# A recurrent cross-attention kernel: one pre-activation bank, dense matmuls at the loop's entry and unread matmul columns in every step

## The chip, the cores and the metric

The kernel runs on one core of a Trainium2 chip. The number that counts is the device time of one execution in microseconds. Three runs of the kernel before gave 1774.48, 1775.82 and 1776.86 us; the median is 1775.82 us.

## What is computed

Two layers act on `x` (4 sequences x 256 positions x 512). Each layer is an attention block and a feed-forward block with residual additions. The first attention block, the dequantized feed-forward block of the first layer and the routed experts of the second are large matrix products. The second layer's attention block is a recurrence over the 256 positions, and it is what the change touches. For each batch row (4) it attends over 64 context positions of 128 features:

```python
def step(carry, tgt):
    s, c, alpha = carry
    f = conv(alpha, conv_w)                                   # 101 taps, 10 channels
    e = einsum('a,bta->bt', va, tanh(enc_proj + (s @ Wa_s.T)[:, None, :] + f @ Wa_f + ba))
    alpha_new = softmax(where(mask, e, -1e30))
    g = einsum('bt,btd->bd', alpha_new, hbatch)
    y = ...                                                   # computed after the loop from kept s and alpha
    rec = tgt @ L_ys.T + s @ L_ss.T + g @ L_gs_w.T + L_gs_b
    ig, fg, cg, og = split(rec)
    c_next = sig(fg) * c + sig(ig) * tanh(cg)
    s_next = sig(og) * tanh(c_next)
```

Each step needs the state `s` and the attention weights of the step before, so 256 steps stand one behind the other.

## The kernel before

The kernel is written engine by engine: each engine has its own instruction list, and counting semaphores (`wait_ge`, `then_inc`) tie them together. Nothing schedules it; the order on each engine is the order of the code. TensorE runs first the attention block, two passes of `gate_up` and `down` for the first feed-forward block with the recurrence's input products in between, then the recurrence loop `pe.Fori(0, S // 2)` with two steps in each turn (`par` 0 and 1, 256 steps in all), and then the expert block.

The numbers of a step in the code, in TensorE's order:

- **The pre-activation** (bank `par`, 128 columns): `context_part` puts the context projection and bias there with three matmuls against the identity (L1181), the convolved attention weights come on top with two float32 matmuls over `uh` and `qv` (L1243), which appear in the trace as four weight loads and four matmuls, and the state part `was2` with `sh` twice and `sl` once (L1193). The state is held in two half-precision pieces, `sh` (high) and `sl` (low). `context_part` and L1243 of step l prepare step l+1: they write bank `1 - par` while the step's own tanh read bank `par`.
- **The state's part of the gates** (L1199): ten matmuls of 4 columns, independent of the attention.
- ScalarE takes tanh of the pre-activation twice (L955 for the high piece `th_hi`, L956 in full precision); VectorE forms the low piece (L746). TensorE forms the scores in bank 2 (L1206, eight matmuls in 32-row groups of outputs, for the maximum, which VectorE reduces at L749) and in bank 3 (L1211, L1213).
- ScalarE's exp (L960, `eh`; L961 in float32), then TensorE's sums over the context: gates (L1221), normaliser (L1227, L1231), and the transform of the attention weights (L1236, L1237). The masks for the next step (L1175, L1176) and `context_part` (L1181) follow at once; they wait for nothing.
- VectorE: reciprocal (L755), products (L760, L769), gate sum `gat` (L771), then two `spread` products (L764), which L1243 waits for (`q0_ready`, `q1_ready`). ScalarE's L963, L964 and L966 and VectorE's L778, L780, L783 make the new state; `sh` releases the next step's L1193, and `sl` (L786) its third matmul.

GpSimd keeps the history (L490, L493) and splits expert weights in the loop. In the trace some names are those of the storage that a tile shares: `krep` stands for `qv` and for the context's gate projection `hg2`, `interT` for the tanh tiles, `s` and `sscale` for the history.

Of the kernel before, what the change touches and what calls it, by code (L numbers as in the profile page):

```python
# [8 lines left out]
ACT = mybir.ActivationFunctionType  # L9
# [7 lines left out]
P = 128  # L17
B, S, H = 4, 256, 512
# [9 lines left out]
J = 64  # L28
KW = 101
FCH = 10  # L30
TH = T // 2
# [46 lines left out]
def build(nc, a, out):  # L78
    with ExitStack() as ctx:
# [32 lines left out]
        identb = sb("identb", [P, P], BF16)  # L112
# [9 lines left out]
        was2 = sb("was2", [J, 2, P], F16)  # L122
# [10 lines left out]
        uh = sb("uh", [P, 2, P])  # L133
        enc = sb("enc", [P, P])
        enc3 = sb("enc3", [P, 3, P], BF16)
# [20 lines left out]
        th = interT[:, 6, 0:P]  # L156
# [686 lines left out]
        def _(act):  # L843
# [107 lines left out]
            with act.Fori(0, S // 2) as i:  # L951
                for par in range(2):
                    l = i * 2 + par
                    act.wait_ge(s["pre_done"], l + 1)
                    nc.scalar.activation(th_hi, bank[par][:, 0:P], ACT.Tanh).then_inc(s["th_s"], 1)  # L955
                    nc.scalar.activation(th, bank[par][:, 0:P], ACT.Tanh).then_inc(s["th_full"], 1)  # L956

                    act.wait_ge(s["et_done"], l + 1)
                    act.wait_ge(s["mx_ready"], l + 1)
                    nc.scalar.activation(eh[:], bank[3][:, 0:8], ACT.Exp, bias=nmx[:, 0:1]).then_inc(s["eh_ready"], 1)  # L960
                    nc.scalar.activation(ex[:, par, :], bank[3][:, 0:8], ACT.Exp, bias=nmx[:, 0:1]).then_inc(s["ex_ready"], 1)  # L961
                    act.wait_ge(s["g_ready"], l + 1)
                    nc.scalar.activation(xs[:, par, 4:12], gat[J:P, :], ACT.Tanh, scale=0.5)  # L963
                    nc.scalar.activation(tfi[:], gat[0:J, :], ACT.Tanh, scale=0.5).then_inc(s["tg_ready"], 1)  # L964
                    act.wait_ge(s["c_ready"], l + 1)
                    nc.scalar.activation(tc_sb[:], xs[:, 1 - par, 0:4], ACT.Tanh, scale=0.5).then_inc(s["tc_ready"], 1)  # L966
# [34 lines left out]
        def _(pe):  # L1001
            mm = nc.tensor.matmul
# [160 lines left out]
                        pass  # L1163

            down(2 * IT0, IT0, wd, B, last_gates)
            pe.wait_ge(s["setup_v"], 1)
            pe.wait_ge(s["mask_ready"], 1)
            pe.wait_ge(s["rin_ready"], 2 * B)
# [6 lines left out]
                mm(bank[2][:, 0:T], bsel[:], maskb[:], start=True, stop=False, skip_group_check=True)  # L1175
                mm(bank[3][:, 0:8], etl[:], etr[:], start=True, stop=False, skip_group_check=True)  # L1176

            def context_part(par):

                for j in range(3):  # L1180
                    mm(bank[par][:, 0:P], identb[:], enc3[:, j, :], start=(j == 0), stop=False, skip_group_check=True)  # L1181

            masks()
            context_part(0)

            with pe.Fori(0, S // 2) as i:
                for par in range(2):
# [2 lines left out]
                    state_part = [(0, sh), (1, sh), (0, sl)]  # L1190
                    for j, st in state_part:
                        pe.wait_ge(s["sl_ready" if st is sl else "sh_ready"], l + 1)
                        last = mm(bank[par][:, 0:P], was2[:, j, :], st[:].unsqueeze(2).broadcast_to([J, B, TH]),  # L1193
                                  start=False, stop=(st is sl), skip_group_check=True)
                    last.then_inc(s["pre_done"], 1)

# [3 lines left out]
                                      start=(j == 0 and st is sh), stop=(j == 1 and st is sl))  # L1200
                    last.then_inc(s["sp_done"], 1)

                    pe.wait_ge(s["th_s"], l + 1)
                    for b in range(B):
                        for h in range(2):
# [6 lines left out]
                    pe.wait_ge(s["th_lo_ready"], l + 1)  # L1212
                    mm(bank[3][:, 0:8], th_lo, vae2[:, 0, :], start=False, stop=True, skip_group_check=True).then_inc(s["et_done"], 1)  # L1213

                    pe.wait_ge(s["eh_ready"], l + 1)

                    def gates(parts, e, first, final):
# [18 lines left out]
                        mm(bank[7][:, 0:8], fwd[:, j, :], eh[:], start=(j == 0), stop=False)  # L1236
                    mm(bank[7][:, 0:8], fwd[:, 0, :], el[:], start=False, stop=True).then_inc(s["ah_done"], 1)  # L1237
                    masks()
                    context_part(1 - par)

                    for h in range(2):
                        pe.wait_ge(s[f"q{h}_ready"], l + 1)
                        mm(bank[1 - par][:, 0:P], uh[:, h, :], qv[:, h, :, :], start=False, stop=False, skip_group_check=True)  # L1243


            pe.wait_ge(s["hist_done"], S)
# [86 lines left out]
```

## Time and profile before

| what | value |
|---|---|
| median of three runs (lowest, highest) | 1775.82 us (1774.48, 1776.86) |
| span of the profiled execution | 1777.0 us, 43152 instructions |
| TensorE busy, weight loads busy | 1506.0 us (85%), 1022.2 us (58%) |
| VectorE, ScalarE, GpSimd busy | 919.2 us (52%), 528.9 us (30%), 387.5 us (22%) |
| recurrence loop, from the first mask matmul to the first matmul behind it | 444.8 to 1603.6 us |
| granted TensorE clock, mean over the span | 0.633 of full speed |

The profile gives no other time for its execution than the span, which is 1.2 us above the median of the runs. The kernel has three stages: up to 444 us the dense part, then 1159 us of recurrence, then some 173 us of experts and output. The page is read by stage: a share of the whole span mixes the three. [...]

### The profile page before, as it was taken

The numbers are of one execution on the slowest core, as the hardware profiler recorded it, in microseconds if no ns is written. First come the engines' busy times: TensorE is split into PE (matmuls) and PEld (weight loads), VectorE is DVE, ScalarE is ACT, GpSimd is POOL, SyncE is SP. The second block draws the span as 40 slices with busy tenths as digits, with TensorE's granted clock in tenths as the row PEclk, the third lists the DMA queues.
The fourth block names the chain that finished last, engine by engine and source line by source line (L and its number), as shares of the span: only waits on it lengthen the run. The fifth ranks groups of instructions, "written<-read, shape, count | busy, mean of one in ns | idle before, by whom it ended". The sixth has DMA issues, their size and how long they took to land.

```text
span 1777.0 us, 43152 instructions
## 1 busy us (share of the span) xinstructions
PE 1506.0 (85%) x15683; PEld 1022.2 (58%) x15683; DVE 919.2 (52%) x4293; ACT 528.9 (30%) x2023; POOL 387.5 (22%) x1030
## 2 busy tenths in 40 slices
PE   6547999999888888888888888888888888887999
PEld 3334454544666666666666666666666666664443
DVE  4996643331555555555555555555555555553422
ACT  1342231221333333333333333333333333331211
POOL 3344321220000222222222222222222222222211
PEclk7658999999555555555555555555555555555999
DMA  8330000001200000000000000000000000000000
GB/s 326 141 115 11 1 1 0 1 1 52 77 0 0 0 0 0 0 0 0 0 0 0 0 0 0 0 0 0 0 0 0 0 0 0 0 0 1 1 24 25
DMA packets 17363, 34.51 MB, mean 19 GB/s; under 512 B 7476, under 2 KB 8675, under 8 KB 17332
## 3 DMA queue, kind: packets, MB, share of 16 engines
q1 hardware_dynamic: 17332, 34.10, 5.3%
q8 instruction: 20, 0.33, 0.1%
q14 instruction: 11, 0.09, 0.0%
HBM read 32.00 MB, written 2.10 MB: 19 GB/s over the span
## 4 chain that ended last, share of the span: by engine, by line
PE 62%; DVE 25%; issue 6%; ACT 5%; POOL 1%; DVEq 1%; SPq 1%; DMA 0%; POOLq 0%; ACTq 0%
PE bank L1243 18%; PE bank L1073 11%; PE bank L1193 6%; PE bank L1088 6%; PE bank L1221 5%; ACT eh L960 4%; DVE interT L746 4%; PE bank L1199 4%; DVE krep L764 3%; PE bank L1213 3%; DVE rinv L755 3%; DVE rs L743 2%; DVE g L760 2%; PE bank L1231 2%; DVE gat L771 2%
## 5 line engine op out<-in xcount | busy, mean ns | idle before, releaser
L1243 PE MATMUL bank<-krep,uh 128*128 128x128 f32 x1024 | 313.1, 461 | 23.6
L1243 PEld LDWEIGHTS bank<-krep,uh 128*128 128x128 f32 x1024 | 237.4, 320 | 92.4 <-DVE krep L764 92.4
L493 POOL TENSOR_TENSOR sscale<-ex,rinv 128x8 f32 x256 | 51.3, 200 | 667.6 <-DVE rinv L755 667.6
L1221 PE MATMUL bank<-eh,krep 128*128 128x4 f16 x2048 | 95.3, 168 | 92.5 <-ACT eh L960 92.5
L764 DVE TENSOR_TENSOR krep<-inv,ahn 128x128 f32<-128x128 f32 x512 | 162.2, 356 | 0.0
L1073 PE MATMUL bank<-xT,wbig 128*128 128x512 f16 x672 | 157.2, 386 | 3.7 <-DVE xT L591 3.7
L743 DVE TENSOR_TENSOR rs<-bank,rin 128x8 f32<-128x8 f32 x256 | 42.8, 167 | 198.1 <-PE bank L1199 198.1
L1221 PEld LDWEIGHTS bank<-eh,krep 128*128 128x128 f16 x2048 | 74.1, 105 | 114.0 <-ACT eh L960 114.0
L963 ACT ACTIVATE xs<-gat 64x8 f32<-64x8 f32 x256 | 53.4, 208 | 288.7 <-DVE gat L771 288.7
L955 ACT ACTIVATE interT<-bank 128x128 f16<-128x128 f32 x256 | 71.2, 278 | 216.9 <-PE bank L1193 216.9
L1181 PE MATMUL bank<-enc,identb 128*128 128x128 bf16 x771 | 128.4, 303 | 0.0
L752 DVE TENSOR_TENSOR el<-ex,eh 128x8 f16<-128x8 f32 x256 | 43.0, 168 | 155.9 <-ACT ex L961 155.9
L1088 PE MATMUL bank<-wbig,interT 128*128 128x512 f16 x504 | 115.5, 387 | 1.4 <-POOL interT L449 1.4
L960 ACT ACTIVATE eh<-bank,nmx 128x8 f16<-128x8 f32 x256 | 68.7, 268 | 155.7 <-PE bank L1213 155.7
L1073 PEld LDWEIGHTS bank<-xT,wbig 128*128 128x128 f16 x672 | 67.0, 102 | 83.3 <-issue 13.5
L1199 PEld LDWEIGHTS bank<-sh,lss 64*128 64x128 bf16 x1536 | 102.4, 114 | 0.0
L1199 PE MATMUL bank<-sh,lss 64*128 64x4 f16 x1536 | 101.3, 170 | 0.0
L1193 PE MATMUL bank<-sh,was 64*128 64x128 f16 x512 | 100.0, 297 | 0.0
L490 POOL COPY sscale<-s 64x4 f32 x256 | 46.4, 181 | 242.8 <-DVE s L784 242.8
L652 DVE SCALAR_TENSOR_TENSOR act_sb<-tanh_sb,bank 128x512 f32<-128x512 f32 x42 | 28.9, 687 | 128.5 <-ACT tanh_sb L895 128.4
L449 POOL TENSOR_TENSOR interT<-act_sb,interT 128x512 f16<-128x512 f32 x42 | 48.9, 1165 | 207.8 <-ACT interT L884 207.8
L1206 PE MATMUL bank<-interT,vah 128*32 128x32 f16 x2048 | 65.5, 198 | 31.3
(201 smaller groups left out, 3044.5 us busy)
## 6 DMA issues: line engine op xcount, KB each, us to landing
wbig<-d_gate_qT SPq DMA_DIRECT2D x4, 896.0 KB, 10.1
wbig<-d_up_qT SPq DMA_DIRECT2D x4, 896.0 KB, 20.7
wbig<-d_down_qT SPq DMA_DIRECT2D x1, 3584.0 KB, 30.5
d_out<-x_sb SPq DMA_DIRECT2D x8, 256.0 KB, 2.0
sscale<-d_gate_sT SPq DMA_DIRECT2D x2, 896.0 KB, 8.6
interT<-d_gate_sT SPq DMA_DIRECT2D x2, 896.0 KB, 14.9
sscale<-d_up_sT SPq DMA_DIRECT2D x2, 896.0 KB, 4.2
interT<-d_up_sT SPq DMA_DIRECT2D x2, 896.0 KB, 4.3
```

The source lines that it names most:

```text
L743: nc.vector.tensor_tensor(rs[:].unsqueeze(1), bank[6][:, 0:8].unsqueeze(1), rin2[:, bass.ds(i, 1), par, :], ALU.add)
L746: nc.vector.tensor_tensor(th_lo, th, th_hi, ALU.subtract).then_inc(s["th_lo_ready"], 1)
L764: return nc.vector.tensor_tensor(qv[:, h, :, :], inv[:].unsqueeze(1).broadcast_to([P, B, TH]), ahn[:, 4 * h:4 * h + 4].unsqueeze(2).broadc ...
L955: nc.scalar.activation(th_hi, bank[par][:, 0:P], ACT.Tanh).then_inc(s["th_s"], 1)
L960: nc.scalar.activation(eh[:], bank[3][:, 0:8], ACT.Exp, bias=nmx[:, 0:1]).then_inc(s["eh_ready"], 1)
L1073: last = mm(bk[:], w[wi][:, kt, it * P:(it + 1) * P], x[xi][:, kt, :], start=(kt == 0 and wi + xi == 0), stop=(kt == KT - 1 and xi == 1))
L1088: last = mm(bank[6 + b % 2][:], i_part[ii][:, it, b * CL:(b + 1) * CL], w[wi][:, it, :], start=(it == 0 and ii + wi == 0), stop=(it == til ...
L1181: mm(bank[par][:, 0:P], identb[:], enc3[:, j, :], start=(j == 0), stop=False, skip_group_check=True)
L1193: last = mm(bank[par][:, 0:P], was2[:, j, :], st[:].unsqueeze(2).broadcast_to([J, B, TH]), start=False, stop=(st is sl), skip_group_check= ...
L1199: last = mm(bank[6][:, 4 * gp:4 * gp + 4], lss3[:, j, gp * P:(gp + 1) * P], st[:], start=(j == 0 and st is sh), stop=(j == 1 and st is sl))
L1221: ins = mm(bank[4][:, 4 * gp:4 * gp + 4], hg2[:, j, h, gp * P:(gp + 1) * P], e[:, 4 * h:4 * h + 4], start=(first and gp == 0 and j == 0 an ...
L1243: mm(bank[1 - par][:, 0:P], uh[:, h, :], qv[:, h, :, :], start=False, stop=False, skip_group_check=True)
```

## The change

Three things change, all on TensorE except the bank that ScalarE reads.

```diff
-                    nc.scalar.activation(th_hi, bank[par][:, 0:P], ACT.Tanh).then_inc(s["th_s"], 1)
-                    nc.scalar.activation(th, bank[par][:, 0:P], ACT.Tanh).then_inc(s["th_full"], 1)
+                    nc.scalar.activation(th_hi, bank[0][:, 0:P], ACT.Tanh).then_inc(s["th_s"], 1)
+                    nc.scalar.activation(th, bank[0][:, 0:P], ACT.Tanh).then_inc(s["th_full"], 1)
...
             down(2 * IT0, IT0, wd, B, last_gates)
+
+            for _ in range(16):
+                mm(bank[1][:], x_part[0][:, 0, 0:P], x_part[0][:, 0, :], start=True, stop=True)
             pe.wait_ge(s["setup_v"], 1)
...
+            def keep_busy(n):
+
+                mm(bank[1][:, 0:n], identb[:], hg2[:, 0].rearrange("p h g -> p (h g)")[:, 0:n], start=True, stop=True)
...
-                        last = mm(bank[par][:, 0:P], was2[:, j, :], st[:].unsqueeze(2).broadcast_to([J, B, TH]),
+                        last = mm(bank[0][:, 0:P], was2[:, j, :], st[:].unsqueeze(2).broadcast_to([J, B, TH]),
...
+                    keep_busy(256)
                     pe.wait_ge(s["th_s"], l + 1)
...
+                    keep_busy(256)
                     pe.wait_ge(s["eh_ready"], l + 1)
...
                     masks()
-                    context_part(1 - par)
+                    context_part()
+                    keep_busy(256)
 
                     for h in range(2):
                         pe.wait_ge(s[f"q{h}_ready"], l + 1)
-                        mm(bank[1 - par][:, 0:P], uh[:, h, :], qv[:, h, :, :], start=False, stop=False, skip_group_check=True)
+                        mm(bank[0][:, 0:P], uh[:, h, :], qv[:, h, :, :], start=False, stop=False, skip_group_check=True)
+                    keep_busy(512)
```

The pre-activation has one bank, bank 0, for all steps. Bank 1 takes results that nothing reads: 16 matmuls of 512 columns between the last input product and the loop, and four `keep_busy` matmuls in each step, of 256, 256, 256 and 512 columns, against the identity. None of them waits for a semaphore. The lists of the other engines keep their order.

TensorE's list at the loop's entry, before; L1009 and L1111 are the last input transposes and products of the recurrence:

```order
L1009 MATMUL bank<-ident,xn 128x128 x4
L1111 MATMUL bank<-sscale,lys 128x128 x8
L1175 MATMUL bank<-maskb,bsel 128x64
L1176 MATMUL bank<-etr,etl 128x8
L1181 MATMUL bank<-enc,identb 128x128 x3
L1186 UNCONDITIONAL_BRANCH
```

And after, where lines 1175, 1176, 1181 and 1186 have become 1178, 1179, 1184 and 1193:

```order
L1009 MATMUL bank<-ident,xn 128x128 x4
L1111 MATMUL bank<-sscale,lys 128x128 x8
L1168 MATMUL bank<-xT 128x512 x16
L1178 MATMUL bank<-maskb,bsel 128x64
L1179 MATMUL bank<-etr,etl 128x8
L1184 MATMUL bank<-enc,identb 128x128 x3
L1193 UNCONDITIONAL_BRANCH
```

The sixteen stand ahead of the semaphore waits that precede the masks. TensorE's list from a step's `context_part` over the step's end into the next step's state part, before:

```order
L1176 MATMUL bank<-etr,etl 128x8
L1181 MATMUL bank<-enc,identb 128x128 x3
L1243 MATMUL bank<-krep,uh 128x128 x2
L1192 REGISTER_ALU
L1193 MATMUL bank<-sh,was 128x128 x2
L1193 MATMUL bank<-sl,was 128x128
L1199 MATMUL bank<-sh,lss 128x4 x3
```

And after (L1188 is `keep_busy`):

```order
L1179 MATMUL bank<-etr,etl 128x8
L1184 MATMUL bank<-enc,identb 128x128 x3
L1188 MATMUL bank<-krep,identb 128x256
L1253 MATMUL bank<-krep,uh 128x128 x2
L1188 MATMUL bank<-krep,identb 128x512
L1199 REGISTER_ALU
L1200 MATMUL bank<-sh,was 128x128 x2
L1200 MATMUL bank<-sl,was 128x128
L1206 MATMUL bank<-sh,lss 128x4 x3
```

The third unread matmul stands between the context part and the float32 pair, the fourth between that pair and the matmuls that the new state releases. TensorE's list around the scores, before:

```order
L1199 MATMUL bank<-sl,lss 128x4 x2
L1206 MATMUL bank<-interT,vah 32x32 x8
L1211 MATMUL bank<-vae,interT 128x8 x2
L1213 MATMUL bank<-vae,interT 128x8
L1221 MATMUL bank<-eh,krep 128x4 x8
```

And after:

```order
L1206 MATMUL bank<-sl,lss 128x4 x2
L1188 MATMUL bank<-krep,identb 128x256
L1214 MATMUL bank<-interT,vah 32x32 x8
L1219 MATMUL bank<-vae,interT 128x8 x2
L1221 MATMUL bank<-vae,interT 128x8
L1188 MATMUL bank<-krep,identb 128x256
L1230 MATMUL bank<-eh,krep 128x4 x8
```

The first unread matmul stands ahead of the wait for tanh, the second ahead of the wait for exp.

## Rows read from the trace of the kernel before

**Rows 1.** The page's forty slices: tenths of full clock, by slice of 44.4 us.

```profile
PEclk7658999999555555555555555555555555555999
```

**Rows 2.** Busy time by stretch: us, each engine's busy time (instructions), clock, DMA share, GB/s.

```profile
26.00:40.00 14.00, 13.35 (x45) 9.99 (x45) 5.10 (x8) 3.81 (x8) 2.08 (x2) 0.50 1.01 420
...
330.00:400.00 70.00, 70.00 (x331) 32.50 (x329) 18.96 (x31) 16.39 (x32) 15.09 (x13) 1.00 0.00 1
...
445.00:446.50 1.50, 1.24 (x29) 0.92 (x27) 0.56 (x3) 0.45 (x2) 0.00 (x0) 1.00 1.03 406
446.50:450.00 3.50, 3.04 (x36) 2.35 (x37) 1.81 (x12) 1.05 (x5) 0.39 (x2) 0.51 1.01 376
...
600.00:1600.00 1000.00, 851.58 (x11500) 646.29 (x11499) 547.66 (x3316) 332.02 (x1549) 214.57 (x774) 0.50 0.00 0
...
1636.00:1641.00 5.00, 5.00 (x11) 1.45 (x11) 0.00 (x0) 0.00 (x0) 0.00 (x0) 0.50 0.00 0
1641.30:1650.00 8.70, 8.70 (x31) 3.04 (x30) 3.38 (x7) 1.28 (x2) 0.94 (x3) 1.00 0.00 0
```

**Rows 3.** Timeline of all engines, one step's state part, scores and exp: start, us, what.

```profile
703.92 0.28 ACT L955 ACTIVATE interT<-bank 128x128 f16<-128x128 f32 x1 [0.85 <-PE bank L1193]
703.94 0.19 PE L1199 MATMUL bank<-sl,lss 64*128 64x4 f16 x2
...
704.25 0.26 PE L1206 MATMUL bank<-interT,vah 128*32 128x32 f16 x8
...
704.61 0.22 DVE L749 TENSOR_REDUCE nmx<-bank 128x1 f32<-128x64 f32 x1
...
704.75 0.19 PE L1213 MATMUL bank<-vae,interT 128*128 128x8 f16 x1
704.98 0.27 ACT L960 ACTIVATE eh<-bank,nmx 128x8 f16<-128x8 f32 x1 [0.61 <-PE bank L1213]
```

**Rows 4.** The same timeline, the same step's later part and the next step's state part.

```profile
705.30 0.37 PE L1221 MATMUL bank<-eh,krep 128*128 128x4 f16 x8 [0.36 <-ACT eh L960]
...
706.16 0.50 PE L1181 MATMUL bank<-enc,identb 128*128 128x128 bf16 x3
...
706.76 0.92 PEld L1243 LDWEIGHTS bank<-krep,uh 128*128 128x128 f32 x4 [0.36 <-DVE krep L764]
706.76 1.22 PE L1243 MATMUL bank<-krep,uh 128*128 128x128 f32 x4
...
707.63 0.15 DVE L783 SCALAR_TENSOR_TENSOR sh<-xs,tc_sb 64x4 f16<-64x4 f32 x1 [0.27 <-ACT tc_sb L966]
...
707.91 0.13 PEld L1193 LDWEIGHTS bank<-sh,was 64*128 64x128 f16 x2 [0.23 <-DVE sh L783]
...
708.10 0.30 PE L1193 MATMUL bank<-sl,was 64*128 64x128 f16 x1
```

**Rows 5.** One line's matmuls at low clock (600 to 1590 us): duration ns min/median/max.

```profile
L1193 PE MATMUL bank<-sl,was x218: 293/304/309, 604.1 to 1585.7; 64*128 64x128 f16 x109
...
L1181 PE MATMUL bank<-enc,identb x657: 287/311/311, 602.1 to 1588.5; 128*128 128x128 bf16 x165
```

**Rows 6.** The same lines at full clock (444 to 447 us).

```profile
L1193 PE MATMUL bank<-sl,was x1: 213/213/213, 445.3 to 445.3; 64*128 64x128 f16 x1
```

**Rows 7.** Timeline at the loop's entry: the last input product, the first masks, the first scores and exp.

```profile
441.58 2.05 PE L1111 MATMUL bank<-sscale,lys 128*128 128x128 f32 x16 [0.69 <-ACT sscale L912]
...
444.82 0.18 PE L1175 MATMUL bank<-maskb,bsel 4*128 4x64 bf16 x1 [1.18 <-issue]
...
445.59 0.28 ACT L955 ACTIVATE interT<-bank 128x128 f16<-128x128 f32 x1 [0.99 <-PE bank L1193]
...
446.64 0.27 ACT L960 ACTIVATE eh<-bank,nmx 128x8 f16<-128x8 f32 x1 [0.60 <-PE bank L1213]
```

**Rows 8.** Dense stages, TensorE timeline: 512-column matmuls, at full clock and at the low one.

```profile
427.27 9.65 PE L1088 MATMUL bank<-wbig,interT 128*128 128x512 f16 x42
...
1636.32 4.02 PE L1073 MATMUL bank<-wbig 128*128 128x512 f16 x9
```

More of the change, by code:

```diff
@@ L1176, in masks, with context_part @@
                 mm(bank[3][:, 0:8], etl[:], etr[:], start=True, stop=False, skip_group_check=True)
-            def context_part(par):
+            def context_part():
                 for j in range(3):
-                    mm(bank[par][:, 0:P], identb[:], enc3[:, j, :], start=(j == 0), stop=False, skip_group_check=True)
+                    mm(bank[0][:, 0:P], identb[:], enc3[:, j, :], start=(j == 0), stop=False, skip_group_check=True)
+            def keep_busy(n):
+                mm(bank[1][:, 0:n], identb[:], hg2[:, 0].rearrange("p h g -> p (h g)")[:, 0:n], start=True, stop=True)
             masks()
-            context_part(0)
+            context_part()
             with pe.Fori(0, S // 2) as i:
@@ L1238, in _ @@
                     masks()
-                    context_part(1 - par)
+                    context_part()
+                    keep_busy(256)
                     for h in range(2):
                         pe.wait_ge(s[f"q{h}_ready"], l + 1)
-                        mm(bank[1 - par][:, 0:P], uh[:, h, :], qv[:, h, :, :], start=False, stop=False, skip_group_check=True)
+                        mm(bank[0][:, 0:P], uh[:, h, :], qv[:, h, :, :], start=False, stop=False, skip_group_check=True)
+                    keep_busy(512)
             pe.wait_ge(s["hist_done"], S)
```

## The prediction

> **What bounds the kernel now.** I read first the page's slices of the granted clock, then busy time by stretch, then the timeline of one step.
>
> The slices show three stages [rows 1]: mixed clock up to slice 8, about half of full speed (1.2 GHz) through the loop, full speed (2.4 GHz) at the end. By stretch, the loop ran at 0.50 through all of 600 to 1600 us, with TensorE recorded busy for 852 us of the 1000 [rows 2]. The fall can be dated: 1.00 from 445 to 446.5 us, 0.51 from 446.5 to 450 us, so within the loop's first step [rows 2]. Before it fell, TensorE had finished the last input product at 443.63 us, stood until 444.82 us, and had then run the first step's small matmuls [rows 7].
>
> A step takes 4.52 us: the third state matmul starts 218 times between 604.1 and 1585.7 us, 981.6 us over 217 steps [rows 5]. 256 of them are 1158 us, two thirds of the time. Every step repeats the same chain, so the timeline of one is enough: state matmuls, tanh (703.92), scores, exp (704.98) [rows 3], sums (705.30), VectorE's products, the float32 pair (706.76), and beside that pair ScalarE's and VectorE's new state, `sh` done at 707.78, with the next state matmuls from 707.91 to 708.40 [rows 4].
>
> Two paths meet at the last point. The state arrives at 707.78. The float32 pair on TensorE ends at 707.98, its records including the passage through the array. Behind exp TensorE starts 0.05 us after its releaser: exp ends 705.25 and L1221 starts 705.30 [rows 3, 4]. Here it starts 0.13 us after. So the pair already holds the state part back by about 0.08 us, and **TensorE has no slack at the end of a step**. Any time put between the pair and the state matmuls moves the end of the step. Elsewhere it has slack: 0.36 us of idle time ahead of L1221, and most of the time between L1181 and L1243 [rows 3, 4].
>
> **The change part by part, with the clock at 1.2 GHz.** A 128-column matmul in a row of several costs (0.50 - 0.29)/2 = 0.105 us here: three L1181 take 0.50 us, the shortest record is 0.287 [rows 4, 5]. Nine of 512 columns took 4.02 us at 0.50, so (4.02 - 0.63)/8 = 0.42 us each [rows 8, 2]. So 256 columns are 0.21 us, 512 columns 0.42 to 0.43.
>
> *One bank.* The writes to bank 0 for step l+1 (`context_part`) stand behind the wait for `eh`, and ScalarE issues `eh` (L960) after both tanh that read the bank. No wait is added and nothing comes later: 0. If reading and rewriting the same bank had a price, it would lie at L1181, which has the room named next.
>
> *First unread matmul, 256 columns, ahead of the wait for tanh.* Behind it are the score matmuls L1206, on TensorE, and VectorE's maximum, which waits for them. L1199's last pair starts at 703.94; its own 4 columns are in the array within some 0.1 us, so the new one streams to about 704.25, where L1206 starts today [rows 3]. It just fits. If it were 0.1 us late, the maximum (ends 704.83) would still be there before exp starts (704.98), which waits for L1213. So 0, bound 0.1.
>
> *Second, 256 columns, ahead of the wait for exp.* L1213 starts 704.75 and L1221 0.55 us later [rows 3, 4]. 0.21 fits: 0.
>
> *Third, 256 columns, behind `context_part`.* L1181 ends at 706.66, the new one at 706.87, and L1243's weights begin to load at 706.76 [rows 4]. Its matmuls need some 0.25 us of loading first, during which another matmul can stream. 0; if weights could not load beside it, 0.11.
>
> *Fourth, 512 columns, behind the float32 pair.* No slack, so all of it counts: the pair's 707.98 becomes 708.41. The three state matmuls, whose operands are all there by then, take 3 x 0.105 = 0.32 behind it, so they end at 708.73 instead of 708.40: **+0.33 us**. That takes the weights of the first state matmul as loaded while the unread one streams, since `sh` is there for TensorE at about 707.83. If they load only after it, another 0.10 us comes on top (a load is 0.1 to 0.13 us): +0.43. I take 0.33, since L1181's loads in a row overlap the streaming in just this way. Tanh, and all behind it, moves with this.
>
> *The sixteen dense matmuls.* At full clock 42 of 512 columns took 9.65 us, 0.23 us each [rows 8], so 16 take 3.6 us. They start where TensorE today stands idle for 1.19 us (443.63 to 444.82, waiting on ScalarE's `rin`) [rows 7]. Net +2.4 us, once.
>
> Sum with the loop at 1.2 GHz: 256 x 0.33 + 2.4 = 86.9 us. On the span of 1777.0 us that is 1863.9; the span stands 1.2 us above the median, so 1862.7, and with the larger price 1775.8 + 256 x 0.43 + 2.4 = 1888.
>
> **The same with the clock at 2.4 GHz.** Then the fourth unread matmul takes 0.21 us and the float32 pair about half of its 1.2 us, so both end before `sh` arrives, and nothing that is added lies on the path. Gains on the path: the `sl` matmul takes 213 ns instead of 304 [rows 5, 6], 0.09 us; from tanh to exp 1.05 us in the first step (445.59 to 446.64) against 1.06 [rows 3, 7], 0.01; the first sum behind exp perhaps 0.02. The rest of the path is ScalarE and VectorE, and matmuls of 4 and 8 columns whose time is passage, not columns. Together 0.12 us of 4.52 (bounds 0.10 and 0.16). So the full clock is worth only 256 x 0.12 = 31 us here: 1775.8 - 31 + 2.4 = 1747 us.
>
> So all hangs on whether the added columns bring the clock up and hold it. If they do, they cost nothing and win 31 us; if not, they cost 85.
>
> **What the rows say on the clock.** Stretches that held 1.00 had TensorE streaming wide matmuls nearly without a break, as 330 to 400 us (331 matmuls in 70 us, 512 columns most of them) [rows 2]. Recorded busy time isn't what counts: from 26 to 40 us TensorE was recorded busy for 13.35 of 14 us, with 45 matmuls among them float32 ones of 128 and 512 columns, and stayed at 0.50 throughout [rows 2]. The rise at 1641 us came after nine unbroken matmuls of 512 columns [rows 2, 8]. In the loop the wide work of a step is, at 1.2 GHz, four float32 passes of 0.21 us, three of `context_part` and three of the state (these over 64 rows) of 0.105 each: 1.5 us of 4.52. The change makes it 2.6 us of 4.85. The last half of a step becomes dense; the first half, from tanh to the sums, gets two blocks of 0.21 us and otherwise keeps matmuls of 4 to 32 columns. At full clock each of these blocks takes half the time, and the share falls to 1.3 us of 4.4. That looks more like the stretches that fell or stayed low than like those that held. The sixteen at the entry should keep the first step or two at 1.00, and then I expect the fall.
>
> [...]
>
> **The rivals.**
>
> *The clock holds (faster).* For it: the added columns lie in four places and fill the longest thin stretches, and the entry is bridged, where the clock fell today. Against it: the density just worked out, and the 26 to 40 us stretch. It gives 1747 us, 1740 to 1752 with the bounds. It decides if the loop's clock reads 0.9 or more.
>
> *The clock goes up and down within the loop.* Where a share p of the steps is at 2.4 GHz, a step costs p x (-0.12) + (1 - p) x 0.33. At p = 0.5 that is +0.105, 1775.8 + 27 + 2.4 = 1805; it breaks even near p = 0.75. For it: the attention stage switches several times, with its mean between the levels [rows 1]. From p = 0.1 to 0.7 it gives 1851 to 1782.
>
> *The columns are free even at 1.2 GHz.* If the float32 pair ended well before `sh`, the fourth block would hide and the time would be 1775.8 + 2.4 = 1778. Against it is the 0.13 us start instead of 0.05. Even then 0.42 us of work would have to fit into less than 0.1.
>
> *The chain behind the state is slower than I think*: weights not loaded ahead, third block in the way. 0.43 + 0.11 per step is 1916 us at most.
>
> **How the numbers follow.** Loop at 1.2 GHz in nearly all steps with 0.33 to 0.43 us on each: 0.70, 1862 us, own range 1848 to 1890. Up and down: 0.12, 1782 to 1851. Clock holds: 0.15, 1747. Free: 0.01. Above 1890: 0.02. The range of 8 in 10 takes the first two: 1782 to 1890. Some 0.2% (3.5 us) is what a measurement of this kernel can tell from no change. Faster: 0.15, and 0.02 from the mixed case beyond break-even, 0.17. Same: 0.02. Slower: 0.81.
>
> **What the changed profile would show.** The clock row of the slices: 5 through the loop, with a 9 or 10 tenths at most in its first microseconds. The step, from one third state matmul to the next, 4.85 us. The state matmuls' releaser no longer VectorE's `sh` but TensorE's own queue, with no idle time ahead of them, and VectorE idle longer before L743 and L746. L1206, L1221 and L1243 at the same distances from tanh as today: 0.33, 1.38 and 2.84 us. The loop's start near 447.2 us. A clock near 1.0 in the loop, a state matmul that still waits for `sh`, or a step under 4.5 us would prove me wrong on the main point; a step near 4.95 only on the weight load.

## The result and the profile after

The changed kernel takes 1899.23 us, median of 4 runs (1897.8 to 1901.57), against 1775.15 us of the kernel before (median of 4, 1773.78 to 1776.86). The ratio is 1.070, with a 95% interval from 1.0685 to 1.0715. It is 124 us slower. The forecast was 1862 us with a range up to 1890: the direction was right, the size was not. The profiled execution of the changed kernel took 1899.79 us, with a span of 1898.0: 1.8 us lie outside that span; with the same 1.8 us the profiled execution of before took, by estimate, about 1779 us, which is 3 us above the median of its runs.

The clock did what was forecast. The page's slices of the changed kernel answer to [rows 1], and the stretches, with columns as in [rows 2], to the rows of the loop there:

```profile
PEclk7559999997555555555555555555555555556999
```

```profile
445.00:447.00 2.00, 1.65 (x36) 1.15 (x35) 0.73 (x4) 0.87 (x4) 0.00 (x0) 1.00 1.03 378
447.00:450.00 3.00, 2.81 (x27) 1.91 (x25) 1.65 (x11) 0.62 (x3) 0.38 (x2) 0.65 1.05 393
...
600.00:1600.00 1000.00, 964.41 (x11199) 651.59 (x11197) 514.35 (x3000) 298.97 (x1400) 194.73 (x702) 0.50 0.00 0
```

From 445 to 447 us TensorE still had a granted clock of 1.00; then, within the first step (0.65 in the mean from 447 to 450 us), it fell to 0.50 and stayed there to the loop's end, with TensorE recorded busy for 964 us of 1000 (before: 852). The trace gives the clock as a share of full speed; what the forecast and the expectations call 1.2 and 2.4 GHz is a share of 0.50 and of 1.00 here. The unread columns raised the busy time and not the clock.

ScalarE's first tanh starts once in each step, so its first and last start give the mean step. The line's summary, kernel before and kernel after (count: duration ns min/median/max, first and last start):

```profile
L955 ACT ACTIVATE interT<-bank x256: 277/278/278, 445.6 to 1599.6; 128x128 f16<-128x128 f32 x128
```

```profile
L955 ACT ACTIVATE interT<-bank x256: 277/278/278, 445.3 to 1720.7; 128x128 f16<-128x128 f32 x128
```

That is (1599.6 - 445.6)/255 = 4.525 us before and (1720.7 - 445.3)/255 = 5.002 us after. The loop explains the whole difference of the spans: its length grows by 1275.4 - 1154.0 = 121.4 us, the span by 121.0. The remainder behind the last tanh is 177.3 us against 177.4. The sixteen dense matmuls took 3.6 us, as forecast, and the masks followed at 444.49 us; the dense stage ahead of them ended 2.5 us earlier than in the trace of before, so their price doesn't show in these two spans. From the last input product to the first mask it is 5.43 us (439.06 to 444.49) against 3.24 before [rows 7]: +2.2 us, where the forecast had 2.4.

The timeline of one step after, columns as in [rows 3] and [rows 4]:

```profile
703.60 1.22 PE L1253 MATMUL bank<-krep,uh 128*128 128x128 f32 x4
...
704.40 0.15 PEld L1188 LDWEIGHTS bank<-krep,identb 128*128 128x128 bf16 x1
704.48 0.15 DVE L783 SCALAR_TENSOR_TENSOR sh<-xs,tc_sb 64x4 f16<-64x4 f32 x1 [0.27 <-ACT tc_sb L966]
...
704.62 0.63 PE L1188 MATMUL bank<-krep,identb 128*128 128x512 f16 x1
...
705.18 0.13 PEld L1200 LDWEIGHTS bank<-sh,was 64*128 64x128 f16 x2 [0.62 <-DVE sh L783]
...
705.72 0.28 ACT L955 ACTIVATE interT<-bank 128x128 f16<-128x128 f32 x1 [1.27 <-PE bank L1200]
...
705.86 0.39 PE L1188 MATMUL bank<-krep,identb 128*128 128x256 f16 x1
...
706.18 0.15 PEld L1214 LDWEIGHTS bank<-interT,vah 128*32 128x32 bf16 x8 [0.22 <-ACT interT L955]
...
706.50 0.23 DVE L749 TENSOR_REDUCE nmx<-bank 128x1 f32<-128x64 f32 x1
...
706.82 0.27 ACT L960 ACTIVATE eh<-bank,nmx 128x8 f16<-128x8 f32 x1 [0.66 <-PE bank L1221]
707.14 0.29 PEld L1230 LDWEIGHTS bank<-eh,krep 128*128 128x128 f16 x8 [0.47 <-ACT eh L960]
...
708.60 0.93 PEld L1253 LDWEIGHTS bank<-krep,uh 128*128 128x128 f32 x4 [0.25 <-DVE krep L764]
```

Two stretches of the step are longer; the others stay within 0.01 us:

| stretch | before | after | difference |
|---|---|---|---|
| load for the float32 pair to load for the state matmuls | 706.76 to 707.91, 1.15 us | 703.60 to 705.18, 1.58 us | +0.43 |
| load for the state matmuls to tanh | 707.91 to 708.44, 0.53 us | 705.18 to 705.72, 0.54 us | +0.01 |
| tanh to exp | 703.92 to 704.98, 1.06 us | 705.72 to 706.82, 1.10 us | +0.04 |
| exp to the first sums | 704.98 to 705.30, 0.32 us | 706.82 to 707.14, 0.32 us | 0 |
| first sums to the float32 pair's load | 705.30 to 706.76, 1.46 us | 707.14 to 708.60, 1.46 us | 0 |

Averaged over all steps, from ScalarE's last tanh of a step (L966) to the next step's first it is 1.480 us against 1.054, and from tanh to exp 1.106 against 1.056: 0.426 and 0.050, together the 0.476 us by which the step grew. The state (`sh`) is ready at 704.63, and its weights load 0.55 us later (before: 0.13), behind a block of columns that nobody reads.

### The profile page after: what moved, and what is told of

Read it like the earlier page. It is cut to its first block, busy times and chain, and to the rows that moved or that the text cites. A ratio compares the mean times of both kernels' runs of the same rounds, so it can differ in the third digit from the quotient of the medians.

```text
span 1898.0 us, 45232 instructions
## 1 busy us (share of the span) xinstructions
PE 1751.8 (92%) x16723; PEld 1104.6 (58%) x16723; DVE 942.4 (50%) x4293; ACT 527.0 (28%) x2023; POOL 387.5 (20%) x1030
## 4 chain that ended last, share of the span: by engine, by line
PE 72%; DVE 16%; ACT 4%; issue 4%; POOL 1%; DVEq 1%; SPq 1%; ACTq 0%; DMA 0%; POOLq 0%
PE bank L1253 15%; PE bank L1073 10%; PE bank L1188 9%; PE bank L1230 6%; PE bank L1200 6%; PE bank L1184 6%; PE bank L1088 6%; ACT eh L960 4%; PE bank L1206 3%; DVE interT L746 3%; DVE nmx L749 3%; DVE rs L743 2%; PE bank L1178 2%; PE bank L1240 2%; PE bank L1054 1%
## 5 line engine op out<-in xcount | busy, mean ns | idle before, releaser
L1188 PE MATMUL bank<-krep,identb 128*128 128x256 f16 (+1 forms) x1024 | 466.4, 455 | 0.0
L955 ACT ACTIVATE interT<-bank 128x128 f16<-128x128 f32 x256 | 71.1, 278 | 328.3 <-PE bank L1200 328.3
L1188 PEld LDWEIGHTS bank<-krep,identb 128*128 128x128 bf16 x1024 | 133.4, 130 | 3.8
L1200 PEld LDWEIGHTS bank<-sh,was 64*128 64x128 f16 x512 | 32.5, 106 | 159.0 <-DVE sh L783 158.9
```

Source lines behind the costliest of these rows:

```text
L955: nc.scalar.activation(th_hi, bank[0][:, 0:P], ACT.Tanh).then_inc(s["th_s"], 1)
L1188: mm(bank[1][:, 0:n], identb[:], hg2[:, 0].rearrange("p h g -> p (h g)")[:, 0:n], start=True, stop=True)
L1200: last = mm(bank[0][:, 0:P], was2[:, j, :], st[:].unsqueeze(2).broadcast_to([J, B, TH]), start=False, stop=(st is sl), skip_group_check=True)
```

## The experiments

Twelve more kernels ran, each compared with the kernel before on the same chip. The kernel before took 1775.2, 1775.1 or 1774.3 us (medians) beside them. The step is again worked out from ScalarE's first and last tanh (L955).

### Which part costs what

Only the blocks and the sixteen matmuls were changed, against the changed kernel. *fourth_only*:

```diff
-            for _ in range(16):
-                mm(bank[1][:], x_part[0][:, 0, 0:P], x_part[0][:, 0, :], start=True, stop=True)
...
-                    keep_busy(256)
                     pe.wait_ge(s["th_s"], l + 1)
...
-                    keep_busy(256)
                     pe.wait_ge(s["eh_ready"], l + 1)
...
                     context_part()
-                    keep_busy(256)
...
                     keep_busy(512)
```

*fourth_256* is the same with `keep_busy(256)` at the end. *first_only* keeps the block ahead of `th_s` alone, *only_second_third* the two of 256 columns ahead of `eh_ready` and behind `context_part()`; neither has the sixteen. *no_blocks* keeps the sixteen and drops all four blocks.

*no_blocks:* 

> One bank and the sixteen dense matmuls at the loop's entry, none of the four blocks in the step. Theory (the blocks cost, clock low): step 4.52 us as before, clock 0.50 in the loop, time 1775 + 2.2 = 1777 to 1778 us; the 2.2 us is the 3.6 us of the sixteen less the idle 1.2 us that they fill, plus what the changed kernel's trace shows behind them. Rival (the single bank costs, because TensorE writes the bank that ScalarE has just read): a good part of the 0.48 us per step is left, some 0.1 us per step or more, 1803 us or more.

*only_second_third:* 

> One bank and the second and third block of 256 columns alone, no dense matmuls at the entry. Theory (both hidden at 1.2 GHz): step 4.52 us, 1775 us, at most 1777. Rival (the third one holds up the float32 pair's weights, 0.02 to 0.11 us a step): 1781 to 1803 us.

*first_only:* 

> One bank and the first block of 256 columns alone (ahead of the wait for tanh), no dense matmuls at the entry. Theory (it delays the score matmuls by 0.13 us, of which 0.04 reach exp through the maximum): step 4.56 us, 1775 + 10 = 1785 us. Rival (it is hidden, the 0.04 comes from elsewhere): 1775 us. Second rival (the delay of the scores counts in full): 1775 + 33 = 1808 us.

*fourth_only:* 

> One bank and the fourth block of 512 columns alone, no dense matmuls at the entry. Theory (its whole 0.43 us is on the path, since the weights of the first state matmul load only when it has streamed): step 4.95 to 4.96 us, 256 x 0.43 to 0.44 = 110 to 113 us over the kernel before, 1885 to 1888 us. Rival (as predicted, weights loaded ahead, and the rest of the 0.48 from the other blocks): step 4.85 us, 1860 us.

*fourth_256:* 

> As fourth_only, with the fourth block cut from 512 to 256 columns. Theory (TensorE has no slack at the end of a step at 1.2 GHz, so the price goes with the columns, 0.107 us for each 128): step 4.73 us, 1775 + 54 = 1829 us. Rival (part of the price of fourth_only is a fixed 0.1 us for a weight load that isn't hidden, the rest the columns): step 4.78 us, 1842 us. Rival (the block eats a slack first): below 4.70 us, below 1820 us.

| kernel | median us | ratio to before (95%) | step us | tanh to exp | L966 to tanh |
|---|---|---|---|---|---|
| before | 1775.2 | | 4.525 | 1.056 | 1.054 |
| no_blocks | 1776.87 | 1.0014 (1.0002 to 1.0025) | 4.518 | 1.051 | 1.056 |
| only_second_third | 1773.86 | 0.9989 (0.9975 to 1.0002) | 4.518 | 1.051 | 1.055 |
| first_only | 1793.42 | 1.0091 (1.0070 to 1.0112) | 4.577 | 1.107 | 1.054 |
| fourth_256 | 1830.11 | 1.0325 (1.0302 to 1.0348) | 4.735 | 1.051 | 1.269 |
| fourth_only | 1884.91 | 1.0617 (1.0599 to 1.0636) | 4.944 | 1.052 | 1.481 |
| the change | 1899.23 | 1.0700 (1.0685 to 1.0715) | 5.002 | 1.106 | 1.480 |

The single bank costs nothing that can be told: no_blocks is 1.7 us slower, no more than the 2.2 us of the sixteen matmuls, and its step is not longer. Nor do the second and third blocks cost anything. The fourth alone is 110 us, and its price goes with its columns: 0.215 us for 256 and 0.427 for 512 in the last column, against 0.424 us from one 512-column matmul to the next at a clock of 0.50, (4.02 - 0.63)/8 of [rows 8], and half of it, 0.212 us, for 256. So no slack eats the first columns and no fixed part comes on top. The first block costs 0.05 us of each step, 13 us, not the 0 that I had given it. The parts add up: 0.051 + 0.427 = 0.478, the change has 0.476.

The first block's mechanism is in its own timeline (first_only, columns as before): the score matmuls start 0.46 us behind tanh instead of 0.33, because they come after the block, and VectorE's maximum ends 1.01 us behind tanh instead of 0.91.

```profile
704.32 0.28 ACT L955 ACTIVATE interT<-bank 128x128 f16<-128x128 f32 x1 [0.85 <-PE bank L1198]
...
704.46 0.39 PE L1186 MATMUL bank<-krep,identb 128*128 128x256 f16 x1
...
704.78 0.15 PEld L1212 LDWEIGHTS bank<-interT,vah 128*32 128x32 bf16 x8 [0.22 <-ACT interT L955]
...
705.10 0.23 DVE L749 TENSOR_REDUCE nmx<-bank 128x1 f32<-128x64 f32 x1
...
705.42 0.27 ACT L960 ACTIVATE eh<-bank,nmx 128x8 f16<-128x8 f32 x1 [0.66 <-PE bank L1219]
```

The maximum ends at 705.33 and exp starts at 705.42. Before it ended 0.15 us ahead of exp, now 0.09. The view puts the wait down to TensorE's L1219, whose record ends at 705.33 too (before, exp started 0.04 us behind that matmul's end). But L1219 starts 0.82 us behind tanh, and its counterpart L1213 started at 0.83: it wasn't delayed, the maximum was. The 0.09 us between maximum and exp is also the median in the changed kernel, even_512, dense and first_512 below, whatever the size of their first block, so it is what lies between the two when exp waits for the maximum. The slack of the maximum was thus some 0.06 us and not 0.15.

first_only as a whole is 18 us slower, more than 255 x 0.051 = 13 us. Its loop took 1167.1 us (+13.1), and the stage behind it 181.6 us against 177.4; there the clock was at 0.87 from 1650 to 1700 us, where the kernel before had 1.00. So 4 us of it, in the profiled execution, belong to how the expert stage's clock came out, not to the block. Why it came out so is open.

### Why the state's weights do not load beside the block

```diff
-                mm(bank[1][:, 0:n], identb[:], hg2[:, 0].rearrange("p h g -> p (h g)")[:, 0:n], start=True, stop=True)
+                mm(bank[1][:, 0:n], identb[0:J, :], hg2[0:J, 0].rearrange("p h g -> p (h g)")[:, 0:n], start=True, stop=True)
```

*fourth_64rows* (J is 64): 

> As fourth_only, with the fourth block over 64 rows of the identity and of its unread operand instead of 128, the same 512 columns. It asks why the first state matmul's weights (64 rows) load only when the block has streamed. Theory (weights of another row count don't load beside a streaming matmul): now the block's own weights start loading only at the end of the float32 pair, and those of the state matmul right behind the block's start, some 0.4 us before it ends; step 4.9 to 5.0 us, since one exposed load takes the place of the other. Rival (the register instruction or the semaphore wait that stands there holds the load back): the state matmul's weights still load at the block's end, and the block's own load beside the pair as in fourth_only.

In the changed kernel the block's weights load at 704.40, while the float32 pair streams, but the state matmul's load starts at 705.18, at the end of the block, though `sh` had been there for half a microsecond. Both other users of that point have 128 rows; the state matmuls have 64. With the block over 64 rows, the weight loads read:

```profile
705.89 0.93 PEld L1248 LDWEIGHTS bank<-krep,uh 128*128 128x128 f32 x4 [0.36 <-DVE krep L764]
707.04 0.10 PEld L1186 LDWEIGHTS bank<-krep,identb 64*128 64x128 bf16 x1 [0.23 <-issue]
707.05 0.11 PEld L1198 LDWEIGHTS bank<-sh,was 64*128 64x128 f16 x1
707.45 0.15 PEld L1198 LDWEIGHTS bank<-sh,was 64*128 64x128 f16 x1 [0.28 <-issue]
```

The block's load now waits until the pair has streamed (707.04), and the state matmul's load follows at 707.05, 0.39 us before its matmul (707.44). Nothing else in the list changed, so neither the semaphore wait nor the register instruction holds the load back; the change from 128 rows to 64 does. The time stays the same, 1884.49 us against 1884.91, step 4.946 against 4.944, since one exposed load took the other's place. So in these traces a load over the same 128 rows starts beside the running matmuls (704.40 in the changed kernel, 0.22 us before its own matmul), and one that goes from 128 rows to 64 does not (705.18, 0.56 us behind the start of a block whose 512 columns take 0.42).

Equal rows alone are not enough either, and this bears on the first block. The weights of the score matmuls are 128 rows by 32 columns of tanh. In first_only tanh is there at 704.60, yet they load at 704.78, which is 0.32 us behind the start of the block of 256 columns; its columns take 0.21 of them, half of the 0.424 us of 512. Before, without a block, they loaded 0.05 us behind tanh. Weights of 128 by 128 did load beside a block, and behind a semaphore wait too, in five_blocks (the kernel is described below):

```profile
703.21 0.29 DVE L746 TENSOR_TENSOR interT<-interT 128x128 f16<-128x128 f32 x1
...
703.41 0.38 PE L1188 MATMUL bank<-krep,identb 128*128 128x512 f16 x1
...
703.56 0.10 PEld L1222 LDWEIGHTS bank<-vae,interT 128*128 128x128 f16 x1
703.62 0.17 PE L1222 MATMUL bank<-vae,interT 128*128 128x8 f16 x1
```

The load waits for VectorE's low piece (703.50) and then starts within 0.06 us, while the 512 columns stream. At a clock of 1.00 these take 0.216 us: the sixteen of the changed kernel took 3.62 us, less the last one's record of 0.38, over 15. So by estimate they stream to 703.63. In these kernels, then, weights loaded beside a streaming matmul when they had its rows and its columns (704.40, 703.56); with 64 rows (705.18), or with 32 columns (704.78), they loaded 0.14 and 0.11 us behind the end of its columns. For the rows an experiment shows it; for the columns it is read from traces, and no run changed them alone.

### Does more density bring the clock up?

```diff
-                    keep_busy(256)
+                    keep_busy(384)
                     pe.wait_ge(s["th_s"], l + 1)
...
+                    keep_busy(384)
                     pe.wait_ge(s["th_lo_ready"], l + 1)
...
-                    keep_busy(256)
+                    keep_busy(512)
+                    keep_busy(512)
                     pe.wait_ge(s["eh_ready"], l + 1)
...
+                    keep_busy(128)
                     pe.wait_ge(s["el_ready"], l + 1)
...
                     context_part()
-                    keep_busy(256)
+                    keep_busy(512)
+                    keep_busy(256)
```

That is *tuned* against the changed kernel. The others differ in the columns of the blocks, in the order of the step:

| kernel | ahead of tanh | ahead of its low piece | ahead of exp | ahead of its low piece | behind the context part | end of step |
|---|---|---|---|---|---|---|
| the change | 256 | | 256 | | 256 | 512 |
| even_512 | 512 | | 512 | | 512 | 512 |
| dense | 768 | | 1024 | | 768 | 512 |
| first_512 | 512 | | 1024 | | 768 | 512 |
| five_blocks | 512 | 512 | 1024 | | 768 | 512 |
| tuned | 384 | 384 | 1024 | 128 | 768 | 512 |

*five_no_entry* is five_blocks without the sixteen.

*even_512:* 

> The changed kernel with four blocks of 512 columns. Theory: too thin to hold the clock, dense enough to raise it at times: loop clock 0.55 to 0.8, steps at the low clock with 0.43 + 0.25 us or so over the kernel before, 1850 to 1910 us. Rival (more columns are better step by step): faster than the changed kernel and clock near 1.00, 1760 us. Rival (clock at 0.50 throughout): step 5.25 us, 1960 us.

*dense:* 

> The changed kernel with the blocks raised from 256, 256, 256, 512 columns to 768, 1024, 768, 512, issued as matmuls of at most 512 columns. Theory (the clock of the changed kernel falls because the half of the step from tanh to the sums stays thin; with streaming in all four gaps it holds): clock 1.00 in the loop, step 4.39 to 4.42 us, since at 2.4 GHz the blocks take 0.32, 0.43, 0.32 and 0.21 us and fit, and the path gains 0.12 us: 1775 + 2.2 - 31 = 1746 us, up to 1754. Rival (the clock stays at 0.50 whatever is added): the blocks stick out by 0.55 us and more on top of 0.48, step 5.5 us, about 2030 us. Rival (up and down): between the two, clock 0.6 to 0.9.

*first_512:* 

> As dense, with the first block cut from 768 to 512 columns and no fifth one. Theory (the first half of the step is the thin one, and dense was only just enough, its clock dipped twice early in the loop): clock below 1.00 in a part of the loop, 0.75 to 0.95, step 4.5 to 4.8 us, 1775 to 1860 us. Rival (the clock holds just as in dense): step 4.45 us, 1759 us.

*five_blocks:* 

> Blocks of 512 ahead of the wait for tanh, a fifth of 512 ahead of the wait for the low piece of tanh (before L1213), 1024 ahead of exp, 768 behind the context part, 512 at the end; sixteen dense matmuls at the entry. Theory (dense kept 1.00 but its first block of 768 delayed the scores by 0.12 us a step; what is taken from it is put where L1213 waits anyway): clock 1.00 in the loop, tanh to exp 1.05 us instead of 1.18, step 4.44 to 4.46 us, so 1775 + 2.2 - 256 x 0.07 = 1759 us, faster than both. Rival (the columns before L1213 delay it and exp too): tanh to exp 1.10 or more, 1772 us or more. Rival (the clock falls again): 1800 us or more.

*five_no_entry:* 

> As five_blocks without the sixteen dense matmuls at the entry. Theory (the loop is dense enough to bring the clock up by itself; the sixteen cost 2.2 us and save one fall): the clock falls after the first step and is back at 1.00 within some 10 us, the two effects about cancel, 1763 to 1768 us. Rival (without the entry the clock stays low, since the blocks make the step long and thin at 1.2 GHz): clock near 0.5, step above 5.3 us, 1980 us.

*tuned:* 

> As five_blocks, with the first block 384 columns instead of 512 and the fifth 384 instead of 512, and 128 columns more ahead of the wait for the low piece of exp (el_ready, L1231). Theory (at 2.4 GHz the score matmuls start when the first block has streamed, 0.44 us behind tanh in five_blocks against 0.33 before): tanh to exp 1.06 to 1.08 us instead of 1.10, clock still 1.00, step 4.44 to 4.45 us, 256 x 0.03 = 8 us under five_blocks, 1757 us. Rival (too thin again in the first half): clock dips, mean 0.9 to 0.98 in the loop, no gain or a loss, 1766 us or more.

| kernel | median us | ratio to before (95%) | step us | tanh to exp | L966 to tanh |
|---|---|---|---|---|---|
| even_512 | 1931.02 | 1.0872 (1.0837 to 1.0907) | 5.118 | 1.294 | 1.414 |
| dense | 1787.81 | 1.0066 (1.0047 to 1.0085) | 4.570 | 1.181 | 0.987 |
| first_512 | 1770.51 | 0.9971 (0.9958 to 0.9983) | 4.486 | 1.078 | 1.006 |
| five_blocks | 1765.68 | 0.9937 (0.9910 to 0.9964) | 4.475 | 1.098 | 0.975 |
| five_no_entry | 1764.23 | 0.9946 (0.9928 to 0.9963) | 4.484 | 1.101 | 0.980 |
| tuned | 1749.48 | 0.9865 (0.9849 to 0.9882) | 4.422 | 1.045 | 0.975 |

The stretch 600 to 1600 us of even_512, dense and five_blocks, one line each in this order, columns as in [rows 2]:

```profile
600.00:1600.00 1000.00, 972.12 (x10935) 599.61 (x10933) 501.79 (x2933) 291.23 (x1368) 189.23 (x685) 0.58 0.00 0
```

```profile
600.00:1600.00 1000.00, 988.01 (x12967) 566.71 (x12965) 567.64 (x3299) 327.62 (x1538) 212.40 (x769) 1.00 0.00 0
```

```profile
600.00:1600.00 1000.00, 995.42 (x13098) 588.47 (x13099) 570.32 (x3335) 331.68 (x1555) 215.33 (x778) 1.00 0.00 0
```

The clock can be held, and the recorded busy time doesn't tell whether it is: 972 us at 0.58, 988 at 1.00. With all four blocks at 512 the clock goes up and down (0.58 in the mean; in stretches of 5 us from 700 to 740 us it is 0.82, six times 0.50, and 0.76), and a step takes 5.118 us against 4.525 before: the worst kernel of all. dense holds but for dips early in the loop (0.51 from 460 to 480 us, 0.98 from there to 600, then 1.00). first_512 dips more often (0.98 in the mean from 800 to 1000 us too), as in the stretch 580 to 612 us:

```profile
580.00:612.00 32.00, 31.70 (x365) 19.44 (x361) 16.13 (x92) 9.34 (x44) 5.85 (x21) 0.63 0.00 0
612.00:800.00 188.00, 186.92 (x2466) 108.72 (x2462) 108.03 (x634) 63.06 (x296) 40.60 (x147) 1.00 0.00 0
```

It is faster than dense all the same, since dense pays for its first block in every step: tanh to exp takes 1.181 us. I had counted dense's blocks as hidden at the clock of 1.00 and expected 1746 us; 768 columns ahead of the scores, by estimate 0.32 us (one and a half times 0.216), are not hidden there. In five_blocks the clock is at 1.00 through the loop, but exp comes 1.098 us behind tanh: the fifth block stands in the way of L1222, whose matmul starts only at 703.62, 0.89 us behind tanh, in the rows above. That is close to the rival in its expectation, 1.10 us or more. tuned cuts both blocks to 384 columns. Parts of one step of tuned:

```profile
704.55 0.16 DVE L783 SCALAR_TENSOR_TENSOR sh<-xs,tc_sb 64x4 f16<-64x4 f32 x1 [0.27 <-ACT tc_sb L966]
...
704.76 0.11 PEld L1200 LDWEIGHTS bank<-sh,was 64*128 64x128 f16 x2 [0.42 <-DVE sh L783]
...
704.81 0.15 DVE L786 TENSOR_TENSOR sl<-s,sh 64x4 f16<-64x4 f32 x1
...
705.02 0.09 PEld L1200 LDWEIGHTS bank<-sl,was 64*128 64x128 f16 x1
705.03 0.23 PE L1200 MATMUL bank<-sl,was 64*128 64x128 f16 x1
...
705.29 0.28 ACT L955 ACTIVATE interT<-bank 128x128 f16<-128x128 f32 x1 [0.77 <-PE bank L1200]
...
705.41 0.34 PE L1188 MATMUL bank<-krep,identb 128*128 128x384 f16 x1
...
705.68 0.13 PEld L1214 LDWEIGHTS bank<-interT,vah 128*32 128x32 bf16 x8 [0.17 <-ACT interT L955]
...
705.98 0.22 DVE L749 TENSOR_REDUCE nmx<-bank 128x1 f32<-128x64 f32 x1
...
706.33 0.27 ACT L960 ACTIVATE eh<-bank,nmx 128x8 f16<-128x8 f32 x1 [0.60 <-PE bank L1222]
```

The scores start 0.39 us behind tanh and the maximum ends 0.13 us before exp, so exp comes 1.04 us behind tanh. At the end of the step the state's load starts 0.05 us behind `sh` (704.71 to 704.76), against 0.13 before, and the `sl` matmul takes 0.23 us instead of 0.30. Only the second of these shortens the step: the `sl` matmul starts 0.32 us behind `sh` in both kernels, since VectorE's low piece of the state is ready only at 704.96, and its load follows 0.06 us later. It was so before:

```profile
707.89 0.15 DVE L786 TENSOR_TENSOR sl<-s,sh 64x4 f16<-64x4 f32 x1
...
708.10 0.10 PEld L1193 LDWEIGHTS bank<-sl,was 64*128 64x128 f16 x1
```

The clock of tuned was at 1.00 from the loop's first step to its last. The kernel is 25 us faster than the one before (ratio 0.9865) and 150 us faster than the change, with the same idea: it differs in where the columns stand and how many there are.

Several times here missed what was expected: even_512 (1931 us, up to 1910 expected), first_512 (1770.5, and a step shorter than the 4.5 us at which the expectation began), five_blocks (1766 against 1759) and tuned (1749.5 against 1757, so better); of the kernels further up, first_only (1793 against 1785).

five_no_entry shows the sixteen dense matmuls to be worth nothing once the loop is dense: the clock fell at the entry (0.74 in the mean over 440 to 460 us), came back by itself and was at 1.00 from 460 us on, and the ratios to the kernel before, 0.9946 and 0.9937, have overlapping intervals.

## The prediction, step by step

**Right: the clock.** It fell in the loop's first step and stayed at 0.50; the sixteen matmuls held it not even for that step. The reason given, that the half of a step from tanh to the sums is thin, fits the runs: first_512 and dense differ in nothing but 256 columns there, and one dips more often than the other; five_blocks, with 512 more than first_512 in the same half, never does (1.00 from 446 to 1586 us). But it is not shown. The columns of a whole step rise in the same order (1280 in the change, 2048 in even_512, 2816 in first_512, 3072 in dense, 3328 in five_blocks), and no run moved columns from one half to the other at the same sum, so whether their place or their number decides stays open.

**Right: what the full clock is worth.** Forecast 0.12 us a step, bounds 0.10 and 0.16, and 1747 us; tuned has 4.525 - 4.422 = 0.103 us and 1749.5 us. The parts fit as well: 0.079 us between L966 and tanh, where 0.09 was forecast for the `sl` matmul, and 0.011 between tanh and exp, where it was 0.01. The 8-column matmul that releases exp, taken as the same at both clocks, has a record of 0.189 us before and 0.179 in tuned. The rival that would have been faster was priced well; it needed other blocks.

**Right: no slack at the end of a step,** read from 0.13 us where 0.05 was usual. fourth_256 and fourth_only have prices that go through zero at no columns. The reason was only half of it: the pair does hold the `sh` weights back by 0.08 us, but the end of the step wouldn't come earlier without that, since `sl` is there only 0.06 us before its own load (708.04 and 708.10).

**Right: one bank, second and third block, 0.** The third was given a bound of 0.11 for a load that can't pass; it was not needed. The 0.25 us of loading ahead of the pair, with which its 0 was argued, is a misreading: the pair's first load and first matmul both start at 706.76 [rows 4].

**Wrong: the fourth block's term.** The step that failed is "That takes the weights of the first state matmul as loaded while the unread one streams", for which I took +0.33 and named +0.43 as the other end. It measured +0.43, and the load started when the block had streamed. The row I leaned on, L1181's loads in a row, is of matmuls of one row count; the state matmuls have another. The rows of before already held the right neighbour: L1193's load started at 707.91, 0.08 us after `sh` could have released it, behind the pair over 128 rows. From the pair's end (707.98) to that of the state matmuls (708.40) they show 0.42 us; the forecast put 0.32 behind the block, and so took away a wait that the kernel before already had. 256 x 0.10 = 25 us.

**Wrong: the first block's term.** "If it were 0.1 us late, the maximum would still be there before exp starts": the scores were 0.13 us late and the maximum 0.10, and the slack of the maximum was 0.06 us, since exp starts 0.09 us behind it at the earliest seen. 0.05 us a step, 13 us. The columns themselves were placed well: the block starts 0.14 us behind tanh and streams 0.21, to 0.35, where 0.33 was forecast. What came on top, 0.11 us, is again weights that did not load beside a streaming block.

**The range.** 25 + 13 = 38 us, within 1 us, is the miss of 1899 against 1862. The range's upper end of 1890 carried only the first of the two, and everything above it had a chance of 0.02. Two small terms that repeat 256 times, both taken at their favourable end, are not independent luck: both rested on the same belief, that weights load while an unread block streams. Of the signs named, the clock row came as forecast; the step is 5.00 us, beyond even the 4.95 that was to tell of the load; and scores, sums and the pair's load stand 0.46, 1.42 and 2.88 us behind tanh, not 0.33, 1.38 and 2.84.

## What to carry to other kernels

In these runs, columns added to hold TensorE's clock had to be free at the granted 0.50 too, or they had to be enough to hold it; in between more of them cost more (1280 in a step, at 0.50, 124 us; 2048 of them, at 0.58, 156 us; 3200 well placed, at 1.00, won 25 us). Put them where the engine provably waits for another, and make each gap's block shorter than the gap at the clock that is in force: the same 512 columns ahead of the state matmuls cost 0.43 us of each step at 0.50, and in tuned, at 1.00, they held nothing up (the state's load starts 0.05 us behind `sh`). Where the next weights have another shape than the block, count their load behind it, as the 64 rows and the 32 columns did here, 0.14 and 0.11 us behind its columns. In a loop of hundreds of steps price every hundredth of a microsecond on the path, and look for the slack of each waiter in its own start behind its releaser, not in the distance to the next instruction.

## What the runs showed of the hardware

Weights for a matmul over 64 rows did not load while one over 128 rows streamed: in the changed kernel the load starts 0.56 us behind the start of the block of 512 columns, which take 0.42. Over the same 128 rows and columns they did load beside it, 0.22 us before their own matmul (704.40 and 704.62). With the block over 64 rows in fourth_64rows the state's load starts 0.39 us before its matmul. Weights of 32 columns waited in the same way in first_only, 0.11 us beyond the 0.21 us of the block's 256 columns.

From one 512-column matmul to the next it is 0.424 us at a clock of 0.50 [rows 8] and 0.216 us at 1.00 (the changed kernel's sixteen).

TensorE's recorded busy time doesn't tell its clock: 964 us of 1000 stood at 0.50 in the changed kernel and 972 at 0.58 in even_512, 988 at 1.00 in dense. A matmul of 8 columns has a record of 0.19 us [rows 3], nearly half as long as one of 256 columns (0.39 us), so records of many small matmuls can fill the time without many columns. At 0.50 a record of 512 columns is 0.63 us, 0.21 more than the step from one to the next. What the forecast calls the passage through the array is this rest of a record; its size was measured, what fills it was not.
